# Moving two kinds of VectorE work in a fused Mamba and attention kernel: x added on TensorE, half of the gates on GpSimd

## The reference

```
# layer 0 (per token t, 512 channels d, 16 states n)
h = h * exp(dt_t * A) + (dt_t * u_t) * B_t          # the recurrence over tokens
y_t = sum_n h * C_t + u_t * D
y   = y * silu(z)                                   # the gate
x   = x + gate_row * (y @ out_proj_w.T)             # out projection, added to x
# layer 1: the same recurrence forwards and backwards on two branches
y1 = silu(mx) * ssm_forward;  y2 = silu(mx) * ssm_backward
x  = x + gate_row * ((y1 + y2) @ Wf.T + bf + skip)
```

## Time and profile before

| | |
|---|---|
| median of 3 runs | 2138.95 us |
| the profiled execution, its own time | 2137.9 us |
| its span, first to last instruction | 2136.1 us |
| mean granted TensorE clock | 0.848 |
| VectorE busy | 1854.2 us, 87% of the span |
| TensorE busy | 1728.3 us, 81% |
| ScalarE busy | 1199.4 us, 56% |
| GpSimd busy | 1147.4 us, 54% |
| chain that ended last, by engine | VectorE 46%, TensorE 33%, issue 10%, ScalarE 5%, GpSimd 4% |

### The profile page before, as it was taken

One profiled execution on the slowest core, in us unless ns is written; L12 is line 12 of the kernel. 1 busy time (PEld: TensorE's weight loads), 2 busy tenths in 40 slices (PEclk: granted clock), 3 DMA queues, 4 the chain that ended last, 5 costly groups with the idle time before them and its releaser, 6 DMA issues.

```text
span 2136.1 us, 22565 instructions
## 1 busy us (share of the span) xinstructions
PE 1728.3 (81%) x7664; PEld 588.8 (28%) x7664; DVE 1854.2 (87%) x2189; ACT 1199.4 (56%) x2147; POOL 1147.4 (54%) x584
## 2 busy tenths in 40 slices
PE   5776979789797777778787878787887899999986
PEld 2221313133231211122221112232663333333323
DVE  4688999899999999999999999999557888888803
ACT  3756565645656565555565655553462266666672
POOL 2667977877888887778888786864000000000000
PEclk9887979859687788878778778797998799999998
DMA  5142222122222222212222222321060522220001
GB/s 197 57 150 71 70 71 78 63 69 67 73 74 80 76 76 79 79 63 74 69 80 75 75 80 79 100 90 54 2 120 30 87 38 31 32 32 2 2 2 40
DMA packets 80727, 143.41 MB, mean 67 GB/s; under 512 B 14587, under 2 KB 19643, under 8 KB 80076
## 3 DMA queue, kind: packets, MB, share of 16 engines
q1 hardware_dynamic: 80612, 141.98, 24.1%
HBM read 132.34 MB, written 9.01 MB: 66 GB/s over the span
## 4 chain that ended last, share of the span: by engine, by line
DVE 46%; PE 33%; issue 10%; ACT 5%; POOL 4%; DMA 1%; SPq 1%; DVEq 0%; ACTq 0%; POOLq 0%
DVE hbuf L2176 27%; DVE hbuf L2161 11%; PE psum L688 6%; PE psum L654 5%; PE psum L674 4%; PE psum L1598 4%; PE psum L569 3%; POOL hbuf L1340 3%; DVE gain L969 2%; PE psum L558 2%; PE psum L1429 1%; PE psum L1405 1%; PE psum L1554 1%; PE psum L1577 1%; PE psum L1456 1%
## 5 line engine op out<-in xcount | busy, mean ns | idle before, releaser
L1340 POOL TENSOR_TENSOR hbuf<-hbuf,cbuf 128x1024 f32<-128x1024 f32 x384 | 902.1, 2356 | 286.6 <-DVE hbuf L2176 147.0
L1968 ACT ACTIVATE psum<-slots,cols 128x512 f32<-128x512 f32 x768 | 525.3, 687 | 450.6 <-DVE hbuf L2176 446.8
L1598 PE MATMUL psum<-hbuf,ident 64*64 64x512 f32 x3072 | 530.1, 768 | 211.6 <-POOL hbuf L1340 211.2
L2161 DVE TENSOR_TENSOR hbuf<-slots,psum 128x1024 f32<-128x1024 f32 x384 | 459.4, 1197 | 52.8 <-POOL slots L1258 30.3
L2176 DVE TENSOR_TENSOR_SCAN hbuf<-psum,hlast,hbuf 128x512 f32<-128x512 f32 x384 | 470.4, 1266 | 3.1 <-ACT psum L1968 3.0
L2176 DVE TENSOR_TENSOR_SCAN hbuf<-psum,hbuf 128x512 f32<-128x512 f32 x384 | 447.4, 1206 | 4.5 <-ACT psum L1968 4.4
L969 DVE TENSOR_REDUCE gain<-psum 128x1 f32<-128x512 f32 x512 | 315.7, 682 | 59.1 <-PE psum L654 58.7
L520 POOL COPY wl<-hbuf 128x512 f32<-128x512 f32 x8 | 4.8, 612 | 429.3 <-PE psum L688 400.7
L654 PE MATMUL psum<-slots 99*128 99x512 bf16 x512 | 197.1, 400 | 23.9 <-DVE gain L969 11.5
L1577 PE MATMUL psum<-bcs,pick 48*128 48x512 bf16 x384 | 171.0, 446 | 45.0 <-DVE hbuf L2161 42.8
L674 PE MATMUL psum<-slots 102*128 102x512 bf16 x512 | 194.4, 388 | 6.5 <-ACT xn_flat L852 1.7
(11 more groups left out here) (267 smaller groups left out, 1943.8 us busy)
## 6 DMA issues: line engine op xcount, KB each, us to landing
cbuf<-scr_c SPq DMA_DIRECT2D x384, 256.0 KB, 3.1
slots<-scr_qk SPq DMA_DIRECT2D x96, 128.0 KB
scr_qk<-slots SPq DMA_DIRECT2D x8, 512.0 KB, 2.8
wl<-in_w SPq DMA_DIRECT2D x1, 3968.0 KB, 12.4
wl<-in_ada_w SPq DMA_DIRECT2D x1, 3584.0 KB
xt<-in_x SPq DMA_DIRECT2D x2, 1024.0 KB, 12.4
wl<-in_w SPq DMA_DIRECT2D x2, 1024.0 KB, 6.5
out<-xt SPq DMA_DIRECT2D x2, 1024.0 KB, 4.7
```

Of the source, the lines that this page charges most:

```text
L1340: pool.tensor_tensor(hs, hs, cbuf[:, at % CRING:at % CRING + 1, :].to_broadcast([P, 2, TC]), ALU.mult).then_inc(weighed, 1)
L1598: last = pe.matmul(psum[side, bank, :], ident[rows_of, rows_of], hbuf[rows_of, at % RING, q, :], start=False, stop=n == NS - 1, skip_group ...
L1968: act.activation(decay_bank(at, q), dts[k % 2][:, e, :], ACT.Exp, scale=coefficient(WORK[k], e, n)).then_inc(decay, 1)
L2161: dve.tensor_tensor(hbuf[:, at % RING, :, :], ws[k % 2][:, 2 * p:2 * p + 2, :], psum[:, 2 + at % 2:3 + at % 2, :].to_broadcast([P, 2, TC]) ...
```

## The change

Three things are done, and the order on each engine is rewritten for them.

1. **The out projections.** Behind each four matmuls TensorE makes a fifth one, the identity times the rows of x, into the same PSUM sums. ScalarE copies the sums over the rows of x (`sums_out`), behind steps 9 and 11 or 6 and 8. VectorE's adds (L2136) are gone. All groups but the decays made ahead are now taken by ScalarE. In layer 1 TensorE now waits for `skip_added`.
2. **The first half's gate.** ScalarE copies the sums of 128x1024 out of PSUM into a new tile `half_sums` (`copy_sums`), behind the decays of step 17 and before what it does beside that step; this frees the banks. GpSimd multiplies the copy by silu of z (`gate_first_half`) after the weighing of step 19. The second half's gate stays on VectorE.
3. **The last out projection** is taken by ScalarE too, behind `exp_keys(0)` of the attention (`take_last_out`).

```diff
-TAKER = ["dve" if key[0] == "out" else "scan" if key[0] == "ahead" else "act" for key in GROUPS]
+TAKER = ["scan" if key[0] == "ahead" else "act" for key in GROUPS]
...
+        half_sums = sb("half_sums", [P, 2, TC])
...
@@ gpsimd
+            def gate_first_half(k):
+
+                z = zs[k % 2][:, 0:2, :]
+                pool.wait_ge(y_free, 2 * k + 1)
+                pool.wait_ge(z_ready, GATED.index(k) + 1)
+                pool.tensor_tensor(z, half_sums[:, :, :], z, ALU.mult).then_inc(gated, 1)
...
+                    if h == NS + 3 and j in GATED:
+                        gate_first_half(j)
                     side.up_to(h)
@@ tensor, project_out
+                pe.wait_ge(gated, GATED.index(k) + 1)
                 pe.wait_ge(y_free, 2 * k + 2)
...
+                if c.layer:
+                    pe.wait_ge(skip_added, 2 * c.b + c.at + 1)
...
                         for e in range(KE):
-                            last = pe.matmul(ps[:, q * D:(q + 1) * D], src[:, e, t0:t0 + P], w_gated[:, e, :],
-                                             start=e == 0, stop=e == KE - 1)
+                            pe.matmul(ps[:, q * D:(q + 1) * D], src[:, e, t0:t0 + P], w_gated[:, e, :],
+                                      start=e == 0, stop=False, skip_group_check=True)
+                        last = pe.matmul(ps[:, q * D:(q + 1) * D], ident[:, :], own_rows(k)[:, 2 * i + q, :],
+                                         start=False, stop=True, skip_group_check=True)
@@ scalar
+            def sums_out(k, at):
+
+                for i in range(2):
+                    yield at + 2 * i
+                    act.activation(own_rows(k)[:, 2 * i:2 * i + 2, :], take("out", k, i).rearrange("p (q d) -> p q d", q=2),
+                                   ACT.Identity).then_inc(taken_act, 1)
...
+            def copy_sums(k):
+
+                n = GATED.index(k)
+                if n:
+                    act.wait_ge(gated, n)
+                act.wait_ge(summed, HALVES * k + NS)
+                act.activation(half_sums[:, :, :], psum[:, 0:2, :], ACT.Identity).then_inc(y_free, 1)
...
+                    if h == NS + 1 and j in GATED:
+                        copy_sums(j)
@@ vector
-                    for i in range(2):
-                        yield start + 2 * i
-                        dve.wait_ge(grouped, done("out", j - 1, i))
-                        xs = own_rows(j - 1)[:, 2 * i:2 * i + 2, :]
-                        dve.tensor_tensor(xs, group_bank(("out", j - 1, i)).rearrange("p (q d) -> p q d", q=2), xs,
-                                          ALU.add).then_inc(taken_dve, 1)
...
-                    if h == NS + 1 and j in GATED:
-                        gate(j, 0)
```

More of the change, by code:

```diff
@@ L492, in sync_attention @@
             sp.wait_ge(y_free, 2 * NK)
-            sp.wait_ge(taken_dve, TAKER.count("dve"))
+            sp.wait_ge(taken_act, taken(G["out", NK - 1, 1]))
             set_ones(1)
@@ L1625, in _ @@
                 pass
-            pe.wait_ge(taken_dve, TAKER.count("dve"))
+            pe.wait_ge(taken_act, taken(G["out", NK - 1, 1]))
             tensor_attention(pe)
@@ L1926, in beside @@
                 if k >= NK:
+                    yield from sums_out(j - 1, 6)
                     yield from attention_inputs()
@@ L1936, in beside @@
                         folded_bias(d)
+                    if j - 1 in GATED:
+                        yield from sums_out(j - 1, 9 if d in (0, 1) else 6)
                     yield 11
@@ L1945, in beside @@
                     turned_out(k)
-                elif c.backward:
+                elif j - 1 in GATED:
+                    yield from sums_out(j - 1, 9)
+                elif c.layer and c.backward:
                     yield from z_out(k, 5, 2)
@@ L2109, in beside @@
                     yield 0
+                    dve.wait_ge(taken_act, taken(G["out", BATCH * CHUNKS + 3, 1]))
                     yield from measure_tokens(tokens_of_batch(0), 5)
@@ L2225, in close_scans @@
             def close_scans():
-                gate(NK - 1, 1)
+                gate_second_half(NK - 1)
             def add_last_out():
-                for _ in beside(NK):
-                    pass
-                dve.wait_ge(taken_dve, TAKER.count("dve"))
+                dve.wait_ge(taken_act, taken(G["out", NK - 1, 1]))
             vector_attention(dve, link, close_scans, add_last_out)
```

30 lines of the change are left out of this document (15 added, 15 removed).

## The result

| | before | changed |
|---|---|---|
| median of 20 runs | 2138.99 us (2134.35 to 2142.84) | 2147.61 us (2134.57 to 2150.11) |
| ratio | | 1.0032, 95% interval 1.002 to 1.0043 |
| the profiled execution, its own time | 2137.9 us | 2141.64 us |
| span | 2136.1 us | 2139.9 us |
| mean granted TensorE clock | 0.848 | 0.850 |

The change makes the kernel slower: the medians stand 8.6 us apart, and the interval of the ratio goes from 0.2 to 0.4%. 3.2 us less were forecast. Seven of the twenty executions lie at or under 2142.8 us, thirteen between 2146.6 and 2150.1. The first profile is one of the lower group, so it can explain only +3.8 us.

What follows compares the result with a forecast made beforehand. VectorE was taken to bound most of the passes, with TensorE or GpSimd bounding in places. Gates -2.3, adds -2.8 and the end +1.9 gave -3.2 us: 2135.8 us on the median's level, range 2128 to 2146 us.

Steps and rivals of the forecast that it cites:

- The gate in pass 2: Pass 2: GpSimd's new multiplication delays the sum of step 20 and all behind it by 2.36 us, 0.2 spare: +2.1 us.
- Passes 10 and 11: Gates there bring 0 us, TensorE's queue being full; pass 11's adds bring -0.4 us.
- the change does not shorten its queue: 0 us: Gates of passes 10 and 11: TensorE runs without gaps from before the gate, so nothing is gained.
- Passes 1, 3, 6, 7: Gates save 1.1 us in each, no wait being near; adds save 1.2 in pass 1, 0.2 in 3, 0.6 in 7.
- Passes 4 and 8: Adds gain 0 us: pass 4 looks like pass 3; in pass 8 VectorE waits for GpSimd's first norm instead.
- The end: Last out projection: four identity matmuls add 2.0 us, ScalarE's copy takes 0.59 for the add's 0.70: +1.9 us, unhidden.
- The sum: Whole kernel: gates -2.3, adds -2.8, end +1.9, together -3.2 us; chance 52%.
- the 52.8 us of waits ahead of loads: VectorE's waits ahead of loads, released by TensorE and GpSimd: taken to show VectorE is not the bound everywhere.
- The whole gain: Rival, 12%: all 17.0 us of VectorE's savings come, less 1.9 at the end: -15.1, 2123.9 us.
- TensorE and GpSimd did not give way: Rival, 18%, that they do: ScalarE frees sums earlier, so passes 2, 10, 11 gain too: -5.4 more, 2130.4 us.
- The slower one: Rival, 16%: GpSimd's multiplication delays step 20's sum in passes 1, 3, 6, 7 too: 9.4 us more, +6.2, 2145.2 us.
- The port lock: Rival, 2%: GpSimd's eight multiplications each stop VectorE's loads for 2.36 us: 18.9 us more, 2154.7 us.

Runs made afterwards that it cites:

- pass2_21: The changed kernel with GpSimd's gate product behind the weighing of step 21 instead of 19 in pass 2 alone: 2137.67 us, ratio 0.9996 to the kernel before.
- adds_only: The changed kernel with both gates on VectorE as before, so only the out projections are changed: 2140.66 us, ratio 1.0014 to the kernel before.
- gates_only: The kernel before with only the first half's gates changed, out projections and VectorE's adds as before: 2141.87 us, ratio 1.0019.
- product_21: The changed kernel with GpSimd's gate product behind the weighing of step 21 instead of 19 in all eight passes: 2139.6 us, ratio 1.0008 to the kernel before.
- no_identity: pass2_21 without the 32 identity matmuls, so x itself is not added: 2138.69 us, ratio 0.9998 to the kernel before.
- gate_pass2: The kernel before with the new first-half gate in pass 2 alone: 2142.07 us, ratio 1.0019.
- products_apart: pass2_21 with GpSimd's four products for the next pass set two behind step 26 and two behind step 27: 2138.05 us, ratio 1.0 to the kernel before.
- delay_before: The kernel before with ten fills of an unread tile on VectorE in pass 3, a pure delay: 2145.22 us, 6.9 more than before.
- selected: The kernel before with new gates in passes 1, 2, 3, 6, 7 and new out projections in 0, 1, 2, 6 only: 2136.53 us, ratio 0.9997.

## Why the prediction was wrong

The step that failed is the price of what is queued on TensorE in two passes: pass 2 was sized at +2.1 - 0.4 us and lost 4.9, and pass 11 was sized at -0.4 us and lost 2.3. These two are 5.9 us of the 7.0 us between forecast and first profile; a third part, the slower executions of the same program, no step had at all.

**The gate in pass 2** was sized at +2.1 us, with the projection behind the late sum at its 3.62 us. The lateness was right to the tenth (2.1 us), and so was the sentence that the gate's own 1.11 us is lost in the longer wait for GpSimd (6.31 for 5.19 us). What failed is the duration of what stands behind: TensorE, which had waited 10.43 and again 1.95 us, ran the sum and the first part of the projection at its lower level (1.99 and 5.30 us for 1.09 and 3.67), and pass 2 lost 4.9 us. pass2_21 shows that both go with the place of the product: 6.2 us back in the pass, and 10 us in the median.

**Passes 10 and 11** were to keep their length or win 0.4 us. Pass 10 did; pass 11 lost 2.2 to 2.4 us in all four profiles of the changed kernel. In the first, the two terms that the prediction had came out: the gate's 1.1 us went and came back as waits at steps 18 to 20 (0 us forecast), and steps 4 to 9 are 0.4 us shorter for the adds. On top come 2.7 us at steps 15 and 16, by TensorE's low level (0.57 granted in the 12 us there, 0.86 in adds_only and gates_only). First the changed kernel, then adds_only:

```profile
1406.90:1418.90 12.00, 10.63 (x36) 4.42 (x32) 10.19 (x10) 4.57 (x7) 7.05 (x3) 0.57 0.28 84
```
```profile
1410.00:1422.00 12.00, 10.64 (x45) 4.76 (x41) 11.63 (x10) 5.81 (x10) 8.29 (x4) 0.86 0.36 87
```

The rule used, "the change does not shorten its queue: 0 us", left out that the same queue has two speeds. Why the level falls earlier here is not shown: the stall is absent with either part of the change alone, and in product_21 and no_identity its part at step 16 is gone (pass 11 at 123.7 and 123.3 us).

**Passes 1, 3, 6, 7**: forecast -2.3, -1.3, -1.1 and -1.7 us, measured -1.5, -1.3, -0.9 and -1.5 us. Passes 4 and 8, forecast 0: +0.3 and -0.2 us. These steps held; in pass 1 the scan of step 18 waits 0.30 us for a decay behind the copy, and that of step 22 waits 1.91 us where before it waited 1.48.

**The end** was +1.9 us, measured +0.5 us for out projection and copy: the identity matmuls took 0.43 to 0.54 us each, 1.85 us in all, but the 32 records of the out projection itself took 8.9 us for 10.2, since the clock came up 4 us after their start, where before it took 6 us. The attention behind it took 0.7 us more; I did not follow it further.

**The sum** of the first profile is then 0.5 (start) + 2.2 (passes) + 1.1 (rest) = +3.8 us against -3.2, and such an execution would have been inside the range. What no step of the prediction had is the second group of executions, which holds the median: 6.2 us more in passes 4, 6 and 9, by the lower level of TensorE's clock. I took one profile of before as the length of every pass, though the changed order can meet other clocks in passes that it doesn't touch. The Trainium skill (TensorE: Matmul & The Clock Gate, "HAM oscillation — how this bites in real kernels") tells of a matmul kernel in which each wait for a DMA leaves the matmuls behind it at the half rate. Here the waits are for GpSimd, and the trace agrees for the long ones (a sum takes 1.98 us behind a wait of 5.07 us, 1.09 us at the full level). In which executions TensorE comes up in time the runs here don't show.

**A row misread.** The prediction took the 52.8 us of waits ahead of loads as a sign that TensorE and GpSimd bound the passes. Of these, GpSimd's 30.3 us are one wait ahead of the very first load; inside the passes it was 22.4 us, all for spreads. The sum did not use the figure.

**The rivals.** The whole gain did not come: VectorE gave up 15.6 us of busy time and waited for others instead. TensorE and GpSimd did not give way either: pass 2 was longer, and pass 10 kept its length. The slower one named the right place, the sum of step 20, but in passes 1, 3, 6 and 7, where it cost nothing. The port lock did not show: the loads took 1194 ns in the three later profiles of the changed kernel, and 1195 to 1196 ns where they overlap one of GpSimd's products (1197 before). In the first profile they took 1208 ns, most in pass 5 (1263 ns), which has no product, and 1206 ns beside the products.

```profile
L2195 DVE TENSOR_TENSOR hbuf<-slots,psum 128x1024 f32<-128x1024 f32 x384 | 458.5, 1194 | 60.9 <-POOL slots L1267 30.3 <-PE psum L1594 30.0
```

**Open.** What decides whether TensorE comes up in time at the starts of passes 6 and 9 and in pass 4, and why it falls earlier in pass 11. The changed kernel missed it in three of four profiles, gate_pass2 met it in its profile, the pure delay missed it in passes 4 and 6. The length of the idle time ahead is not enough (products_apart), the change itself isn't needed (delay_before), and there is one profile only of the kernel before. Nor is it shown why the attention is 3.2 to 3.3 us shorter in the profiles of selected and delay_before, with no edit in it.

## What to carry to other kernels

Where work is moved to an engine whose queue is on the bound, the step at which it stands counts more than its length: in pass 2 a product of 2.4 us cost some 5 us, and two steps later it was free; in passes 1 and 7 it was the other way round, and the later place cost 2.3 and 1.4 us. Price what is queued behind a delayed matmul at both levels of TensorE's clock. And where profiles of one kernel differ by more than the change is to bring, take several and compare them pass by pass before a difference of medians is explained.

## What the hardware showed that I had not expected

- The same program runs in two groups of lengths, with no execution between 2142.7 and 2146.6 us. Three places of 1.5, 2.1 and 2.6 us make up 6.2 us between their profiles: in the first 12 us of pass 9, the same instructions of TensorE ran at 0.50 or 0.76 granted clock.
- A delay of 5.4 us costs 6.9 us in the median of one kernel and about 2 us in that of its neighbour (five executions each).
- Removing 32 matmuls from TensorE (no_identity) made passes 3 and 11 and the end shorter, four passes longer, and the median no shorter.
- The length of a wait alone does not tell the level behind it: in products_apart a sum took 1.98 us behind a wait of 2.92 us and 1.99 us behind one of 1.88 us, and in pass 7 of the changed kernel one took 1.09 us behind a wait of 2.31 us.
